# Turning y by DMA from SBUF to SBUF, in place of TensorE transposes, in a fused attention and FFN kernel

## What is computed

```python
x = x + matmul(fake_quant(layernorm(x)), fake_quant(ctx))       # per batch entry: 512x1024 by 1024x1024
y = layernorm(x)
logits = y @ W_router.T                                         # 8 experts
top-2 of softmax(logits), renormalised -> combine               # [rows, 8], two entries not zero
h = einsum('nd,erd->ner', y, A_stack) * combine[..., None]      # rank 16 for each of 8 experts
x = x + y @ W_base.T + b_base + 2.0 * einsum('ner,eor->no', h, B_stack)
```

## Time and profile before

| | |
|---|---|
| time, median of 3 runs | 176.6 us (176.6 to 176.65) |
| time of the profiled execution | 176.58 us |
| its span, first to last instruction | 174.8 us |
| PE busy | 164.2 us, 94% |
| DVE busy | 117.9 us, 67% |
| ACT busy | 73.9 us, 42% |
| POOL busy | 59.8 us, 34% |

### The profile page before, as it was taken

One profiled execution on the slowest core, in us unless ns is written; L12 is line 12 of the kernel. 1 busy time (PEld: TensorE's weight loads), 2 busy tenths in 40 slices (PEclk: granted clock), 3 DMA queues, 4 the chain that ended last, 5 costly groups with the idle time before them and its releaser, 6 DMA issues.

```text
span 174.8 us, 2640 instructions
## 1 busy us (share of the span) xinstructions
PE 164.2 (94%) x970; PEld 89.2 (51%) x970; DVE 117.9 (67%) x276; ACT 73.9 (42%) x100; POOL 59.8 (34%) x140
## 2 busy tenths in 40 slices
PE   6988889899989898999999999999999999999992
PEld 3542435345535373645565565564664555556541
DVE  7993749999989999997459238518707906624812
ACT  3096519799978976124252033205205205200000
POOL 8905476888820000583630720540310130000000
PEclk9999999999999999999999999999999999999999
DMA  5999999999910000002002003001100200200211
GB/s 105 375 417 410 410 409 406 411 407 412 401 57 2 0 4 0 0 0 120 4 2 120 0 0 121 3 0 55 68 0 0 120 0 4 120 0 0 120 62 60
DMA packets 6780, 22.74 MB, mean 130 GB/s; under 512 B 880, under 2 KB 1136, under 8 KB 6768
## 3 DMA queue, kind: packets, MB, share of 16 engines
q1 hardware_dynamic: 6624, 22.58, 33.2%
q10 hardware_dynamic: 144, 0.00, 0.0%
HBM read 18.38 MB, written 4.19 MB: 129 GB/s over the span
## 4 chain that ended last, share of the span: by engine, by line
PE 73%; DVE 15%; issue 3%; POOL 3%; ACT 3%; DVEq 0%; ACTq 0%; POOLq 0%
PE ps L805 43%; PE ps L765 10%; PE ps L795 6%; PE ps L774 4%; PE ps L756 2%; DVE xs L519 2%; PE ps L788 2%; PE ps L786 2%; PE ps L787 2%; ACT w_hi L357 2%; DVE w_lo L584 2%; DVE ident L660 2%; PE ps L750 1%; DVE bnx L450 1%; DVE bnx L448 1%
## 5 line engine op out<-in xcount | busy, mean ns | idle before, releaser
L805 PE MATMUL ps<-w_hi,yt_hi 128*128 128x512 f16 x128 | 39.5, 380 | 1.7 <-DVE w_lo L584 1.1
L805 PE MATMUL ps<-w_lo,yt_hi 128*128 128x512 f16 x128 | 39.4, 379 | 0.0
L805 PE MATMUL ps<-w_hi,yt_lo 128*128 128x512 f16 x128 | 39.4, 379 | 0.0
L765 PE MATMUL ps<-a,a_t 128*128 128x512 f16 x128 | 31.2, 379 | 1.9 <-DVE a_t L512 1.1
L318 ACT ACTIVATE a<-stage,prm,inv_s 128x1024 uint8<-128x1024 f32 x16 | 19.5, 1240 | 10.1 <-POOL a L232 6.1
L384 ACT ACTIVATE gate<-gate,ar_undo 128x1 f32<-128x1 f32 x8 | 2.4, 295 | 48.5 <-DVE gate L613 48.5
L612 DVE MAX8 top<-ps 128x8 f32<-128x8 f32 x8 | 1.4, 173 | 31.0 <-PE ps L788 31.0
L805 PEld LDWEIGHTS ps<-w_hi,yt_lo 128*128 128x128 f16 x128 | 12.5, 98 | 15.1
L805 PEld LDWEIGHTS ps<-w_lo,yt_hi 128*128 128x128 f16 x128 | 12.5, 98 | 14.8
L765 PEld LDWEIGHTS ps<-a,a_t 128*128 128x128 f16 x128 | 11.9, 98 | 15.8 <-DVE a_t L512 2.6
L237 POOL TENSOR_TENSOR xs<-xs,corr 128x1024 f32<-128x1024 f32 x5 | 11.8, 2359 | 22.2 <-DVE b_lo L590 22.2
(11 more groups left out here) (133 smaller groups left out, 277.2 us busy)
## 6 DMA issues: line engine op xcount, KB each, us to landing
stage<-in_ctx_kv SPq DMA_DIRECT2D x16, 512.0 KB, 13.4
stage<-in_w_t SPq DMA_DIRECT2D x8, 512.0 KB, 10.6
xs<-in_x SPq DMA_DIRECT2D x7, 512.0 KB, 13.6
out_dram<-xs SPq DMA_DIRECT2D x7, 512.0 KB, 2.7
ar_raw<-in_ar_t SPq DMA_DIRECT2D x1, 544.0 KB, 15.6
xs<-in_x SPq DMA_DIRECT2D x2, 256.0 KB, 3.9
b_raw<-in_b_t SPq DMA_DIRECT2D x1, 512.0 KB, 11.3
bias_sb<-in_bias SPq DMA_DIRECT2D x1, 512.0 KB, 12.0
```

The source lines that it names most:

```text
L765: last = nc.tensor.matmul(ps[:, s1_bank(t) + h, :], a1_t[:, t % 4, k, :], a2[:, n, h * H:(h + 1) * H], start=k == 0, stop=k == K - 1)
L805: ins = nc.tensor.matmul(ps[:, OUT_BANK[p] + h, :], part, rhs[:, k, h * H:(h + 1) * H], start=k == 0 and part is hi and rhs is w_hi, stop= ...
```

## The change

Tiles 0 and 1 stay as they were. For tiles 2 to 7, y is split into its two fp16 halves while it still lies by token rows, and each half, 128x1024 in fp16, is turned by one DMA from SBUF to SBUF, issued by SP. ACT's `round_y` writes `y_hi`, DVE's `rest_y` writes `y_lo` = y - `y_hi`; both lie in slots 0 and 1 of `a1_t`, which stage 1 no longer needs. On ACT, `sum_row` moves behind `split_hct`; on DVE, `rest_y` stands ahead of `statistics_y`, where `split_yt` stood behind it. PE waits for both DMAs ahead of `narrow`.

```diff
@@ SP
+            def transpose_y(t):
+                sp.wait_ge(out_done, t - 1)
+                sp.wait_ge(y_hi_ready, t - 1)
+                sp.dma_start_transpose(out=yt_hi[:, t % 2, :, :], in_=y_hi).then_inc(y_hi_turned, 16)
+                sp.wait_ge(y_lo_ready, t - 1)
+                sp.dma_start_transpose(out=yt_lo[:, t % 2, :, :], in_=y_lo).then_inc(y_lo_turned, 16)
...
             for t in range(T - 1):
+                if t + 2 < T:
+                    transpose_y(t + 2)
                 sp.wait_ge(out_summed, t + 1)
                 sp.dma_start(out_tiles[t], xs[:, t, :]).then_inc(stored, 16)
@@ ACT
             def make_y(t):
                 act.wait_ge(y_scaled, t + 1)
                 if t > 0:
-                    act.wait_ge(y_transposed, t)
+                    act.wait_ge(y_transposed, min(t, 2))
+                if t > 2:
+                    act.wait_ge(y_lo_ready, t - 2)
...
+            def round_y(t):
+                if t > 2:
+                    act.wait_ge(y_hi_turned, 16 * (t - 2))
+                act.wait_ge(stage1_done, T)
+                act.wait_ge(y_ready, t + 1)
+                nc.scalar.activation(y_hi, y[:, :], ACT.Copy).then_inc(y_hi_ready, 1)
...
                 gate_weight(t)
                 if t + 1 < T:
                     make_y(t + 1)
-                    sum_row(t + 1)
+                    round_y(t + 1)
                 split_hct(t)
                 if t + 1 < T:
-                    split_yt(t + 1)
+                    sum_row(t + 1)
@@ DVE
+            def rest_y(t):
+                dve.wait_ge(stage1_done, T)
+                dve.wait_ge(y_ready, t + 1)
+                dve.wait_ge(y_hi_ready, t - 1)
+                if t > 2:
+                    dve.wait_ge(y_lo_turned, 16 * (t - 2))
+                nc.vector.tensor_tensor(y_lo, y[:, :], y_hi, ALU.subtract).then_inc(y_lo_ready, 1)
...
                 add_bias(t)
+                if t + 1 < T:
+                    rest_y(t + 1)
                 if t + 2 < T:
                     statistics_y(t + 2)
-                if t + 1 < T:
-                    split_yt(t + 1)
@@ PE
             for t in range(1, T - 1):
-                pe.wait_ge(yt_lo_ready, t + 1)
+                if t == 1:
+                    pe.wait_ge(yt_lo_ready, 2)
+                else:
+                    pe.wait_ge(y_hi_turned, 16 * (t - 1))
+                    pe.wait_ge(y_lo_turned, 16 * (t - 1))
                 narrow(t)
...
                     if k == 2:
                         transpose_hc(t)
-                    if k == (5 if t == 1 else 3):
-                        transpose_y(t + 1)
                     if k == 5:
                         lora(t)
...
-            pe.wait_ge(yt_lo_ready, T)
+            pe.wait_ge(y_hi_turned, 16 * (last - 1))
+            pe.wait_ge(y_lo_turned, 16 * (last - 1))
             narrow(last)
```

More of the change, by code:

```diff
@@ L62, in xattn_ffn @@
         a1_t = sb("a1_t", [P, 4, K, P], F16)
+        y_hi = a1_t[:, 0, :, :].rearrange("p k c -> p (k c)")
+        y_lo = a1_t[:, 1, :, :].rearrange("p k c -> p (k c)")
         corr = sb("corr", [P, B, D], F32)
@@ L168, in xattn_ffn @@
         y_scaled, y_ready, y_transposed = sem("y_scaled"), sem("y_ready"), sem("y_transposed")
+        y_hi_ready, y_lo_ready, y_hi_turned, y_lo_turned = (sem(n) for n in ("y_hi_ready", "y_lo_ready",
+                                                                             "y_hi_turned", "y_lo_turned"))
         first_half_hi, first_half_lo = sem("first_half_hi"), sem("first_half_lo")
```

## The result

The changed kernel takes 171.81 us (171.81 to 171.84, 4 runs), the kernel before 176.6 (176.56 to 176.65). The ratio is 0.9729, 95% interval 0.9712 to 0.9746: 2.7% faster, inside the range given and 0.6 us under the 172.4 forecast. The span fell from 174.8 to 170.0 us.

The account below looks back on a forecast made before the run. PE was taken to bound stage 2, so its removed transposes come off and its new waits come on: 176.6 - 5.14 + 0.9 (wait at tile 2) = 172.4 us, range 171.3 to 184.

Parts of the forecast that it names:

- What bounds, and what is removed: Stage 2: PE bounds; tiles 2 to 7 lose their transposes on PE, 0.79 + 5 x 0.87 = 5.14 us off.
- The room: From the end of `rest_y` to PE's next first weight load: 4.24 us at tiles 3 to 7, 2.7 at tile 2.
- The same formula: Kernel time as 176.6 - 5.14 + max(0, X - 2.7) + 5 x max(0, X - 4.24).
- X: Time from the end of `rest_y` until PE may load its first weights of the next tile; 3.6 us chosen.
- the upper bound: Low half's DMA: eight block commands at 0.43 us each, the last 7 x 0.43 = 3.0 us later, X = 5.1.
- The lower bound of 2.1: Low half's DMA: no quicker than a plain DMA of the same 256 KB from SBUF, 2.1 us to landing.
- rival 2: Each transpose paced block by block, X from 4.9 to 6.3, PE gaps at every tile, 185.4 us at 6.3; chance 0.29.
- The wait at tile 2: PE waits 0.9 us for the low half's DMA at tile 2, and for nothing at tiles 3 to 7.
- What I had costed at nothing: Later `statistics_y`, SP's waits, stores and `sum_row` were to move without adding time.
- the 2.3 us of cover: Of 4.4 us between POOL having y's bias ready and ACT using it, about 2.3 are left.
- rival 3: Eight blocks one after another with whole latency, 15.2 us for a half, kernel near 305 us; chance 0.09.

## Why the prediction was right

**What bounds, and what is removed.** Right, and 0.1 us too small. Between tiles it was 0.87 by first products (14.16 to 13.29), as forecast. At tile 2 I had 0.79. From tile 1's first product to tile 2's it is 14.19 us before and 13.30 in the kernel with the low half and POOL's sum both moved, in which nothing waits, so the transposes cost 0.89 there as well: 5.24 us in all for 5.14. The kernel with transposes kept gives all of it back. To price eight overlapping matmuls by the start of the next work, and not by the 1.04 that they show, was what made the sum close.

**The room.** Right: 4.24 at tiles 3 to 7, where tile 6 shows 139.74 - 135.52 = 4.22, and 2.7 at tile 2, where it is 86.16 - 83.53 = 2.63 by the first load of that same kernel. The same formula, fed with the X of each run, gives 171.9 for the changed kernel (X = 3.16; measured 171.81), 174.9 for one more transpose (4.56; 174.29) and 183.1 for two more (5.92; 183.46). It is a little too strict, since I counted to the first weight load: when PE doesn't wait, its first product starts 0.21 behind that load, when it waits only 0.03 behind it, so some 0.18 of each wait costs nothing. In the run with two more, the dip of the clock (1.29 us) hides that the formula is too strict.

**X.** The mechanism was right, the size was off: 3.16 for 3.6. And 3.6 was no measurement but the middle of two bounds. Any X up to 4.24 gives a time between 171.5 and 173.0 by my own sum, so the time came out well because the room was right; that X came near was in part luck. The term that failed is the upper bound, "a command for each block at the pace of one issue", 0.43 us for each further block: the issue is 1.24 us for four blocks or eight, and what grows with the blocks is the transfer, by 0.16 us each. The lower bound of 2.1, from a store to HBM, was low too; a copy from SBUF to SBUF of that size lands after 2.3. And rival 2's lower end should have read 5.1, which is 2.1 + 7 x 0.43, and not 4.9.

**The wait at tile 2.** 0.9 forecast, 0.36 measured by first products (13.66 us from tile 1 to tile 2, for 13.30 without a wait). The cast adds 0.08 behind it (13.37 from tile 2 to tile 3, for 13.29). So the sum that closes is 176.6 - 0.89 - 5 x 0.87 + 0.36 + 0.08 = 171.8. Of the 0.6 us between this and the 172.4 forecast, 0.54 is the shorter wait and 0.1 the transposes of tile 2, less the 0.08 of the cast.

**What I had costed at nothing.** Stores and `sum_row` moved without a price, as said; the stores beside the transposes land after 3.0 us and not 2.7, which nothing waits for. The statistics moved almost without one: of the 2.3 us of cover forecast for y at tile 6 there are 2.36. One thing I had missed. The later statistics made POOL's `scale_y` 1.3 us later in tile 2, and that pushed `add_corr` from 86.59 to 87.86, into the gate of that tile. It costs 0.05 us as the kernel stands, and hides 0.4 from whoever mends the other wait.

**The rivals.** Block by block (rival 2) and blocks in series (rival 3) are both out by the landing, 3.0 us for eight blocks. The 1309 ns that the Trainium skill ("VectorE: DVE Perf Modes", The three transpose paths) has for one 128x128 block is no price for each of several: eight land in 3.0 us.

## What to carry to other kernels

Price work on a full engine by the start of what follows it, and price a new wait by two times: when its last input is written, and when the waiting engine would come to it. Then the answer to "is it hidden" is a difference (here 4.24 us against 3.16), and a kernel with one more transfer tests it. Where a transposing DMA replaces transposes on PE, use one large DMA for each operand and make its input early in its engine's order: here the order on DVE was worth 2.4 us and that on ACT 0.9, while putting the low half ahead of `add_bias` as well gave nothing by itself. When a wait is removed and the time stays, read the next wait on the same engine before giving the edit up; the second here was held by POOL, whose program the change leaves as it is and only shifts in time.

## What the runs showed of the hardware

- A DMA transpose of 128x1024 fp16 from SBUF to SBUF: 1.24 us of the issuing queue, 3.0 us to landing; a plain copy 0.47 and 2.3. Of 128x512: 1.25 and 2.4. In both kinds, data moves from 1.1 to 1.2 us after the issue begins; the transfer keeps the DMA engines busy for 1.4 us with the turn and 0.7 without.
- Issued behind one another the transposes start 1.27 to 1.38 us apart, each issue overlapping with the transfer before it.
- Twelve of them beside a busy PE cost no measurable time (0.9997, 0.9988 to 1.0006). Six stores beside them landed after 3.0 us, where 2.7 was usual.
- A cast of 8 numbers in each row on DVE took 0.4 to 1.7 us, ending 0.02 to 0.03 us behind a POOL sum of 128x1024 that had started ahead of it; with that sum moved, 0.17.
- Around one wait of PE of 2.95 us the granted clock was at the lower level from 88.8 to 92.2 us, and the tile took 1.3 us more. Around waits of 1.4 to 1.7 us there was no dip.
